# Linear-attention kernel: the value products cut into 64 by 32 pieces on eight array tiles, the state product's loops turned

## The chip, the cores and the metric

The kernel runs on one core of one Trainium2 chip. The metric is the device time of one execution in microseconds (us). The three runs of the kernel before took 1104.5, 1074.18 and 1075.11 us, median 1075.11 us. The profiled execution is a further run with its own time.

## The reference

The input is x of 8 sequences, 1024 tokens and 512 channels in fp32. The block is

```
x = x + attn(layernorm(x));   x = x + ffn(layernorm(x))
attn: q, k, v = split(x @ W_attn + b_attn), 16 heads of 32
      q = elu(q) + 1;  k = elu(k) + 1
      token by token:  kv += k_t (outer) v_t;  ksum += k_t
                       y_t = (q_t @ kv) / (q_t . ksum + 1e-6)
      return y @ W_proj + b_proj
ffn:  x and weight clipped to +-448 and rounded to fp8 e4m3, then x @ weight.T + bias
```

So attention is causal and linear: a token's output is its query times the running sum of the outer products of keys and values.

## The kernel before

**Tiling.** The 8192 tokens are 64 steps of 128 tokens (`NT` = 64, 8 steps to a sequence, `PER` = 8). Step n has two halves of 64 tokens, a = 0 and 1. A block is four steps; the projection to q, k and v of block j+1 is computed while block j's attention runs. The 16 heads stand as 4 groups g of 4 rows h: head 4g+h has its 32 channels on partitions 32h to 32h+31 of `qk[:, g, :]`.

**One step on TensorE (PE),** in the order that the loop at line 390 gives it: `scores(n)` (k times q within each half), `from_state(n)` (q times what was summed before the half: `state` for half 0, `mid` for half 1), two of the block-ahead projections of 12 matmuls each (`ahead`), four transposes of keys (`k_tokens(n+1)`), the third projection, `values(n)` (masked scores times v), `update(n+1)` (keys times values of the next step, into `mid` and `state`), `proj(n-1)`, `ffn(n-2)`. The last four steps (`tail(n)`) have no projection ahead.

**The small products.** Scores, state product, values and update are fp32. Each such matmul of the program stands in the profile as two LDWEIGHTS and two MATMUL instructions; the text calls one LDWEIGHTS with its MATMUL a pair. The array is cut into tiles by the partitions that the operands come from (rows) and those that the result goes to (columns):

| product | line | array tile | tiles in use | pairs in a step | columns streamed |
|---|---|---|---|---|---|
| scores | 305 | 32 by 64 | 8 | 64 | 64 |
| state product | 320 | 32 by 64 | 4 at a time (a is the outer loop) | 64, or 32 in a sequence's first step | 33 |
| values | 337 | 64 by 64 | 2 of 4 (half a from rows of half a to columns of half a) | 64 | 33 |
| update | 290 | 64 by 32 | 8, or 4 where only `mid` is made | 64 or 32 | 33 |

The 33rd column of v is 1, so that column 32 of each result is the denominator. `S` has four PSUM banks, one for each h; the scores of row h stand in its columns 0 to 255, and `Y`, the sums of state product and values, in columns 256 to 387 of the same bank. In every bank partition p of `Y` is token p of the step.

**After the values** DVE (line 640 to 650) adds 1e-6 to the denominators, takes the reciprocal and multiplies all of `Y` into `y`, in one instruction of 128 by 512; the next `scores` waits for it (`s_y`). ACT and POOL split `y` into two fp16 parts, and a transposing DMA brings them to `yt` for `proj`. After `proj` come DVE's sum and statistics (L661, L578 to L583), POOL's normalization (L838, L840), ACT's rounding to fp8 and a transposing DMA `x2t<-x2b` (L953), for which `ffn` waits. All DMAs are issued by SP in one order. The masks of the scores run on DVE (L618) and by ACT and POOL; `values` waits for both.

Almost all matmuls are recorded at line 212, the helper `matmul`, so they are told apart by their tiles.

Of the kernel before, what the change touches and what calls it, by code (L numbers as in the profile page):

```python
# [5 lines left out]
ALU = mybir.AluOpType  # L6
# [11 lines left out]
P = 128  # L18
HALF = P // 2
W = 33  # L20
# [28 lines left out]
def state_count(n):  # L49

    return n + 1 - (n + 1) // PER


def tail(n):
    return n >= NT - 4


def masked_dve(n):

    return n + 1 if not tail(n) else NT - 4 + 2 * (n - NT + 4) + 2  # L60
# [15 lines left out]
def build(nc, x_d, wa_d, ba_d, wp_d, bp_d, wf_d, bf_d, out_d):  # L76
    ctx = ExitStack()
    with ctx:
        def sb(name, shape, dt):
            return ctx.enter_context(nc.sbuf_tensor(name, shape, dt))  # L80
# [4 lines left out]
        def sem(name):  # L85
            return ctx.enter_context(nc.semaphore(f"s_{name}"))
# [10 lines left out]
        sm = sb("sm", [P, 4, 4, HALF], F32)  # L97

        state = sb("state", [P, 2, 4 * W], F32)
        mid = sb("mid", [P, 4 * W], F32)  # L100
        den = sb("den", [P, 16], F32)
        y = sb("y", [P, D], F32)
# [27 lines left out]
        Y = S[:, :, 4 * HALF:4 * HALF + 4 * W]  # L130
# [33 lines left out]
        s_mid, s_state, s_den, s_dinv, s_y, s_ytl = sem("mid"), sem("state"), sem("den"), sem("dinv"), sem("y"), sem("ytl")  # L164
# [20 lines left out]
        def parts(n):  # L185
            j, c = divmod(n, 4)
            return qk[j % 2], v1[j % 2], j, c

        def tokens(n, a):

            c = n % 4
            return slice(c * P + a * HALF, c * P + (a + 1) * HALF), slice(a * HALF, (a + 1) * HALF)

        block = ctx.enter_context(nc.Block())

        @block.tensor
        def _(e):
# [13 lines left out]
            def matmul(out, a, b, start, stop):  # L211
                return e.matmul(out, a, b, start=start, stop=stop, skip_group_check=True)  # L212
# [94 lines left out]
            def from_state(n):  # L307

                src, v, j, c = parts(n)
                first = n % PER == 0  # L310
                pe.wait_ge(s_mid, n + 1)
                if not first:
                    pe.wait_ge(s_state, state_count(n - 1))
                for a in range(1 if first else 0, 2):
                    cols, out = tokens(n, a)
                    held = mid if a else state[:, n % 2, :]
                    for g in range(4):
                        for h in range(4):
                            rows = slice(32 * h, 32 * h + 32)
                            mm = matmul(Y[out, h, g * W:(g + 1) * W], src[rows, g, cols], held[rows, g * W:(g + 1) * W],  # L320
                                        g == 0, False)
                            if a == 1 and g == 3:
                                mm.then_inc(s_score, 1)

            def values(n):
                src, v, j, c = parts(n)
                first = n % PER == 0
                pe.wait_ge(s_smd, masked_dve(n))
                if not tail(n):
                    pe.wait_ge(s_sel, n + 1)  # L330
                pe.wait_ge(s_v, n + 1)
                pe.wait_ge(s_one, 2)
                for h in range(4):
                    for g in range(4):
                        for a in range(2):
                            rows = tokens(n, a)[1]
                            mm = matmul(Y[rows, h, g * W:(g + 1) * W], sm[rows, h, g, :], v[rows, c, 4 * g + h, :],
                                        first and a == 0 and g == 0, True)
                mm.then_inc(s_av, 1)

            def t_y(n):
# [48 lines left out]
            for n in range(NT + 2):  # L390
                j, c = divmod(n, 4)
                if n < NT:
                    scores(n)
                    from_state(n)
                    ahead(j + 1, 3 * c)
                    ahead(j + 1, 3 * c + 1)
                if n <= NT and tail(n - 1):
                    t_y(n - 1)
                if n < NT:
                    if n + 1 < NT:  # L400
                        k_tokens(n + 1)
                    ahead(j + 1, 3 * c + 2)
                    values(n)
                    if n + 1 < NT:
                        update(n + 1)
                if 1 <= n <= NT:
                    proj(n - 1)
                if n >= 2:
                    t2(n - 2)
                    ffn(n - 2)  # L410
# [163 lines left out]
        def _(e):  # L574
# [59 lines left out]
            def values(n):  # L634

                out = Y.rearrange("p h (g w) -> p h g w", w=W)
                inv = den[:, :].rearrange("p (h g) -> p h g", h=4).unsqueeze(3)
                dve.wait_ge(s_av, n + 1)
                dve.wait_ge(s_y, n)
                e.tensor_scalar(inv, out[:, :, :, 32:33], DEN_EPS, None, ALU.add).then_inc(s_den, 1)  # L640
                dve.wait_ge(s_den, n + 1)
                e.reciprocal(den[:, :], den[:, :]).then_inc(s_dinv, 1)
                dve.wait_ge(s_dinv, n + 1)
                if tail(n - 1):
                    dve.wait_ge(s_ty, n - NT + 4)
                elif n:
                    dve.wait_ge(s_yl, n)
                    dve.wait_ge(s_yh, n)
                e.tensor_tensor(y[:, :].rearrange("p (h g i) -> p h g i", h=4, g=4), out[:, :, :, 0:32],  # L649
                                inv.broadcast_to([P, 4, 4, 32]), ALU.mult).then_inc(s_y, 1)  # L650

            def t_y(n):
                dve.wait_ge(s_yth, n - NT + 5)
# [149 lines left out]
            for n in range(NT + 2):  # L803
                j, c = divmod(n, 4)
                if n < NT:
                    if n + 8 < NT:
                        ln1(n + 8)
                    scores(n)
                    ahead(j + 1, 3 * c)
                    if n == 1:  # L810
                        ffn_sum()
                    if n + 8 < NT:
                        ln1_parts(n + 8)
                    ahead(j + 1, 3 * c + 1)
                if n <= NT and tail(n - 1):
                    t_y(n - 1)
                if n < NT:
                    if n == 0:
                        proj_weight()
                    ahead(j + 1, 3 * c + 2)  # L820
                    if n == 0:
                        ffn_high()
                    values(n)
                    if n + 1 < NT:
                        update(n + 1)
                    if n == 0:
                        ffn_round()
                if 1 <= n <= NT:
                    proj(n - 1)
                if n >= 2:  # L830
                    ffn(n - 2)
# [193 lines left out]
```

## Time and profile before

| | us |
|---|---|
| median of 3 runs | 1075.11 |
| profiled execution, its time | 1077.97 |
| profiled execution, its span | 1076.2 |
| PE busy | 1048.8 (97% of the span) |
| PE weight loads busy | 616.9 (57%) |
| DVE busy | 648.9 (60%) |
| ACT busy | 458.3 (43%) |
| POOL busy | 534.8 (50%) |

The granted clock of TensorE was 0.99 of full speed over the span. Busy time of PE is the time in which at least one matmul is under way; small matmuls overlap, so a stage's cost is read in the timeline, from its first start to the next stage's first start. In a timeline row the second number runs from the first start to the last end of the group.

### The profile page before, as it was taken

What the parts mean: (1) busy time and instruction counts of PE and PEld (TensorE: products, weight loads), DVE (VectorE), ACT (ScalarE), POOL (GpSimd) and SP (SyncE); (2) the same over time, 40 slices, a digit from 0 to 9 for tenths busy, and PEclk for the clock granted to TensorE, in tenths of its full rate; (3) what the DMA queues carried; (4) which work ended last, traced back from release to release, by engine and by line L of the source; (5) the groups of instructions that cost most, each with busy time, mean ns of one, the idle gap of its engine ahead of it and who ended that gap; (6) DMA issues with size and microseconds to landing.
All of it is one profiled execution on the core that took longest, in us unless ns stands there. A gap on an engine that the chain in (4) does not pass through costs nothing.

```text
span 1076.2 us, 43457 instructions
## 1 busy us (share of the span) xinstructions
PE 1048.8 (97%) x19504; PEld 616.9 (57%) x19504; DVE 648.9 (60%) x1319; ACT 458.3 (43%) x715; POOL 534.8 (50%) x524
## 2 busy tenths in 40 slices
PE   5989999999999999999999999999999999999996
PEld 3456555556556556556555555555555655655663
DVE  6666666666666566565665656566565656644454
ACT  5633452533534353452534444353452534434222
POOL 3445665554554454554455454455455455443233
PEclk9989999999999999999999999999999999999997
DMA  8615333333324324224333234333323433221121
GB/s 270 92 34 84 80 66 81 81 73 79 75 71 81 75 66 91 71 66 86 75 78 79 70 70 83 75 76 81 70 72 84 71 81 76 61 61 46 32 58 45
DMA packets 185354, 82.51 MB, mean 77 GB/s; under 512 B 165840, under 2 KB 165840, under 8 KB 185168
## 3 DMA queue, kind: packets, MB, share of 16 engines
q1 hardware_dynamic: 185168, 79.73, 33.5%
q8 instruction: 153, 2.51, 1.0%
q14 instruction: 33, 0.27, 0.1%
HBM read 22.81 MB, written 16.78 MB: 37 GB/s over the span
## 4 chain that ended last, share of the span: by engine, by line
PE 93%; DVE 2%; POOL 1%; ACT 1%; issue 1%; DMA 1%; POOLq 0%
PE R L212 70%; PE S L212 21%; PE R L216 3%; POOL st L838 1%; DVE st L578 0%; POOL xn L840 0%; DMA x2t<-x2b 0%; DVE xs L661 0%; DVE sm L618 0%; POOL xnhl L853 0%; DMA xs<-in_L_attn_x 0%; DVE wl L716 0%; DVE raw L755 0%; ACT qk L426 0%; ACT wh L417 0%
## 5 line engine op out<-in xcount | busy, mean ns | idle before, releaser
L212 PE MATMUL R<-xt,wh 128*128 128x512 f16 x1024 | 307.1, 382 | 2.4 <-ACT wh L417 2.4
L601 DVE SCALAR_TENSOR_TENSOR qk<-qk,rel 128x512 f32<-128x512 f32 x128 | 131.1, 1025 | 170.1 <-ACT rel L429 170.0
L872 POOL TENSOR_TENSOR yhl<-y,yhl 128x512 f16<-128x512 f32 x60 | 70.1, 1168 | 322.0 <-ACT yhl L417 322.0
L212 PE MATMUL R<-xt,wl 128*128 128x512 f16 x512 | 194.3, 381 | 0.0
L838 POOL TENSOR_TENSOR st<-st,half 128x1 f32<-128x1 f32 x128 | 94.1, 735 | 187.8 <-DVE st L583 175.3
L212 PE MATMUL R<-wh,xt 128*128 128x512 f16 x512 | 161.5, 382 | 0.0
L212 PEld LDWEIGHTS R<-xt,wh 128*128 128x128 f16 x1024 | 96.9, 98 | 108.7 <-DVE xt L709 2.6
L426 ACT ACTIVATE qk<-R,bqk,wm 128x512 f32<-128x512 f32 x128 | 99.5, 777 | 121.4 <-PE R L212 121.3
L212 PEld LDWEIGHTS S<-v,sm 64*64 64x64 f32 x4096 | 124.5, 135 | 28.6 <-issue 25.4
L212 PE MATMUL R<-wph,yt 128*128 128x512 f16 x512 | 132.9, 382 | 2.0 <-DVE yt L654 2.0
L212 PE MATMUL S<-v,sm 64*64 64x33 f32 x4096 | 131.6, 221 | 2.3 <-DVE sm L618 2.3
L661 DVE SCALAR_TENSOR_TENSOR xs<-R,wm,xs 128x512 f32<-128x512 f32 x64 | 48.1, 751 | 106.3 <-PE R L212 106.3
L417 ACT ACTIVATE yhl<-y 128x512 f16<-128x512 f32 x60 | 37.8, 631 | 165.5 <-DVE y L649 165.5
L860 POOL TENSOR_TENSOR xs<-xs,bp 128x512 f32<-128x512 f32 x64 | 107.3, 1682 | 0.0
L417 ACT ACTIVATE o<-R 128x512 f16<-128x512 f32 x64 | 38.2, 597 | 156.2 <-PE R L212 156.2
L429 ACT ACTIVATE rel<-R,bqk,wm 128x512 f32<-128x512 f32 x128 | 98.5, 769 | 0.0
L595 DVE TENSOR_TENSOR xnhl<-xn,xnhl 128x512 f16<-128x512 f32 x56 | 86.3, 1540 | 19.5 <-ACT xnhl L417 19.5
L212 PE MATMUL R<-wl,xt 128*128 128x512 f16 x256 | 97.7, 381 | 0.0
L578 DVE BATCH_NORM_STATS2 st<-xs 128x6 f32<-128x512 f32 x128 | 88.4, 691 | 6.2 <-DMA xs<-in_L_attn_x 3.9
L212 PEld LDWEIGHTS R<-xt,wl 128*128 128x128 f16 x512 | 50.4, 98 | 61.4 <-issue 1.7
L881 POOL TENSOR_TENSOR xs<-xs,bf 128x512 f32<-128x512 f32 x64 | 81.0, 1266 | 5.3
L212 PEld LDWEIGHTS R<-wh,xt 128*128 128x128 f16 x512 | 50.3, 98 | 56.4 <-issue 1.6
(90 smaller groups left out, 1440.7 us busy)
## 6 DMA issues: line engine op xcount, KB each, us to landing
xs<-in_L_attn_x SPq DMA_DIRECT2D x64, 256.0 KB, 3.4
out<-xs SPq DMA_DIRECT2D x64, 256.0 KB, 2.5
raw<-in_L_attn_W_attn SPq DMA_DIRECT2D x3, 1024.0 KB, 9.3
xs<-in_L_attn_W_proj SPq DMA_DIRECT2D x4, 256.0 KB
raw<-in_L_ffn_weight SPq DMA_DIRECT2D x1, 1024.0 KB, 16.4
x2t<-x2b SPq DMA_TRANSPOSE x62, 2.4
xt<-xnhl SPq DMA_TRANSPOSE x60, 3.2
yt<-yhl SPq DMA_TRANSPOSE x60, 3.3
```

The lines of the kernel that those rows point to most:

```text
L212: return e.matmul(out, a, b, start=start, stop=stop, skip_group_check=True)
L417: return e.activation(out, in_, ACT.Copy, **more)
L426: e.activation(dst[:, i, :], bank["qkv", j, i][:, :], ACT.Exp, scale=UN[i // 4], bias=bqk[:, i:i + 1])
L429: e.activation(rel[:, u % 2, :], bank["qkv", j, i][:, :], ACT.Relu, scale=UN[i // 4], bias=bqk[:, i:i + 1]).then_inc(s_relu, 1)
L578: e.bn_stats(row[:, 0:6], src).then_inc(s_bn, 1)
L595: e.tensor_tensor(xnhl[:, m % 4, 1, :], xn[:, m % 2, :], xnhl[:, m % 4, 0, :], ALU.subtract).then_inc(s_xlo, 1)
L601: e.scalar_tensor_tensor(qk[j % 2][:, i, :], qk[j % 2][:, i, :], 1.0, rel[:, (u - 1) % 2, :], ALU.min, ALU.add).then_inc(s_phi, 1)
L661: e.scalar_tensor_tensor(x, bank["proj", n][:, :], UN_P, x, ALU.mult, ALU.add).then_inc(s_x1, 1)
L838: e.tensor_tensor(row[:, 10:11], row[:, 9:10], half[:, :], ALU.pow).then_inc(s_rs, 1)
L860: e.tensor_tensor(x, x, bp[:, :], ALU.add).then_inc(s_xb, 1)
L872: e.tensor_tensor(yhl[:, n % 2, 1, :], y[:, :], yhl[:, n % 2, 0, :], ALU.subtract).then_inc(s_yl, 1)
L881: e.tensor_tensor(x, x, bf[:, :], ALU.add).then_inc(s_x1b, 1)
```

## The change

`values` cuts each product of 64 tokens by 64 columns of the array into two of 64 by 32, so it has 128 pairs in a step instead of 64. For the odd rows h = 1 and 3 the halves change places in `Y`: half 0's results go to partitions 64 to 127, half 1's to 0 to 63 (`valued`). Four groups of pieces in turn then use all eight tiles of 64 by 32. `from_state` writes to the same swapped places, and its loops are turned: g is outermost and the halves alternate within it, so that eight tiles of 32 by 64 are in use. DVE's multiplication, which has to bring the odd rows' halves back, becomes three instructions: one of 128 partitions by 256 elements for h = 0 and 2, and two of 64 partitions by 256.

```diff
+        def valued(a, h):
+            b = (a + h) % 2
+            return slice(b * HALF, (b + 1) * HALF)
...
-                for a in range(1 if first else 0, 2):
-                    cols, out = tokens(n, a)
-                    held = mid if a else state[:, n % 2, :]
-                    for g in range(4):
+                for g in range(4):
+                    for a in range(1 if first else 0, 2):
+                        cols = tokens(n, a)[0]
+                        held = mid if a else state[:, n % 2, :]
                         for h in range(4):
                             rows = slice(32 * h, 32 * h + 32)
-                            mm = matmul(Y[out, h, g * W:(g + 1) * W], src[rows, g, cols], held[rows, g * W:(g + 1) * W],
-                                        g == 0, False)
+                            mm = matmul(Y[valued(a, h), h, g * W:(g + 1) * W], src[rows, g, cols],
+                                        held[rows, g * W:(g + 1) * W], g == 0, False)
...
-                for h in range(4):
+                for h in (0, 2):
                     for g in range(4):
-                        for a in range(2):
+                        for a, i in ((0, h), (1, h), (0, h + 1), (1, h + 1)):
                             rows = tokens(n, a)[1]
-                            mm = matmul(Y[rows, h, g * W:(g + 1) * W], sm[rows, h, g, :], v[rows, c, 4 * g + h, :],
-                                        first and a == 0 and g == 0, True)
+                            for at in range(0, HALF, 32):
+                                out = valued(a, i).start + at
+                                mm = matmul(Y[out:out + 32, i, g * W:(g + 1) * W], sm[rows, i, g, at:at + 32],
+                                            v[rows, c, 4 * g + i, :], first and a == 0 and g == 0, True)
...
-                e.tensor_tensor(y[:, :].rearrange("p (h g i) -> p h g i", h=4, g=4), out[:, :, :, 0:32],
-                                inv.broadcast_to([P, 4, 4, 32]), ALU.mult).then_inc(s_y, 1)
+                dst = y[:, :].rearrange("p (h g i) -> p h g i", h=4, g=4)
+                e.tensor_tensor(dst[:, 0:4:2, :, :], out[:, 0:4:2, :, 0:32],
+                                inv[:, 0:4:2, :, :].broadcast_to([P, 2, 4, 32]), ALU.mult)
+                for a in range(2):
+                    at, to = valued(a, 1), tokens(n, a)[1]
+                    made = e.tensor_tensor(dst[to, 1:4:2, :, :], out[at, 1:4:2, :, 0:32],
+                                           inv[at, 1:4:2, :, :].broadcast_to([HALF, 2, 4, 32]), ALU.mult)
+                made.then_inc(s_y, 1)
```

## Rows read from the trace of the kernel before

**Rows 1.** The page: span, then line, engine, operation, tiles, count, busy us, mean ns, idle.

```profile
span 1076.2 us, 43457 instructions
...
PE 1048.8 (97%) x19504; PEld 616.9 (57%) x19504; DVE 648.9 (60%) x1319; ACT 458.3 (43%) x715; POOL 534.8 (50%) x524
...
PE R L212 70%; PE S L212 21%; PE R L216 3%; POOL st L838 1%; DVE st L578 0%; POOL xn L840 0%; DMA x2t<-x2b 0%; DVE xs L661 0%; DVE sm L618 0%; POOL xnhl L853 0%; DMA xs<-in_L_attn_x 0%; DVE wl L716 0%; DVE raw L755 0%; ACT qk L426 0%; ACT wh L417 0%
...
L212 PE MATMUL S<-v,sm 64*64 64x33 f32 x4096 | 131.6, 221 | 2.3 <-DVE sm L618 2.3
```

**Rows 2.** Timeline of PE, one step: start us, us until the group's last end, what.

```profile
499.88 2.06 PE L212 MATMUL S<-v,sm 64*64 64x33 f32 x64
501.86 0.76 PE L212 MATMUL R<-v,ktok 64*32 64x33 f32 x64
502.55 1.04 PE L212 MATMUL R<-wph,yt 128*128 128x512 f16 x4
```

**Rows 3.** Weight loads of S that began by a time, counted (x) from 499.80.

```profile
499.80:500.20 0.40, 0.33 (x12) 1.00 0.54 105
499.80:501.20 1.40, 1.33 (x46) 1.00 0.62 135
```

**Rows 4.** Timeline of PE in 0.07 us at the start of the values.

```profile
499.88 0.25 PE L212 MATMUL S<-v,sm 64*64 64x33 f32 x2
```

**Rows 5.** Weight loads of the update, counted (x) from 501.80.

```profile
501.80:502.01 0.21, 0.15 (x33) 1.00 1.09 146
501.80:502.16 0.36, 0.30 (x36) 1.00 0.86 137
501.80:502.31 0.51, 0.45 (x54) 1.00 0.71 120
```

**Rows 6.** Timeline of PE, scores and state product of the same step.

```profile
506.11 0.85 PE L212 MATMUL S<-qk 32*64 32x64 f32 x60
...
507.73 0.61 PE L212 MATMUL R<-xt,wh 128*128 128x512 f16 x2
```

**Rows 7.** Weight loads of S in that stretch, counted (x) from 506.10.

```profile
506.10:506.51 0.41, 0.40 (x37) 1.00 0.00 0
506.10:506.71 0.61, 0.60 (x61) 1.00 0.00 0
```

**Rows 8.** Timeline of PE, a sequence's first step, without the state.

```profile
184.29 0.91 PE L212 MATMUL S<-qk 32*64 32x64 f32 x64
185.00 0.67 PE L212 MATMUL S<-mid,qk 32*64 32x33 f32 x32
185.60 0.60 PE L212 MATMUL R<-xt,wh 128*128 128x512 f16 x2
```

**Rows 9.** Timeline of DVE behind the values.

```profile
501.98 0.18 DVE L640 TENSOR_SCALAR den<-S 128x16 f32<-128x16 f32 x1 [1.25 <-PE S L212]
...
502.48 0.69 DVE L649 TENSOR_TENSOR y<-S,den 128x512 f32<-128x512 f32 x1
...
503.40 0.30 DVE L632 TENSOR_TENSOR state<-R,mid 128x132 f32<-128x132 f32 x1
```

**Rows 10.** Issues of x2t over 490 to 990 us.

```profile
L953 SPq DMA_TRANSPOSE x2t<-x2b x31: 1188/1222/1232, 499.2 to 982.7; - x31
...
DMA to landing us min/median/max: 2.3/2.5/4.3
```

**Rows 11.** Timeline, an issue of x2t by SP, and the next ffn on PE.

```profile
516.72 1.22 SPq L953 DMA_TRANSPOSE x2t<-x2b  x1
...
521.32 1.03 PE L212 MATMUL R<-wft,x2t 128*128 128x512 bf16 x4
```

**Rows 12.** Timeline of PE, the last steps, and what ended its idle time.

```profile
1024.09 2.06 PE L212 MATMUL S<-v,sm 64*64 64x33 f32 x64 [0.78 <-DVE sm L618]
...
1029.78 1.04 PE L212 MATMUL R<-wft,x2t 128*128 128x512 bf16 x4 [0.24 <-DMA x2t<-x2b]
...
1033.81 2.06 PE L212 MATMUL S<-v,sm 64*64 64x33 f32 x64 [0.35 <-DVE sm L618]
```

## Prediction

> **What bounds the kernel now.** I read the page's engine totals first: PE is busy for 97% of the span, DVE for 60%, the others less, and the chain that ended last runs through PE's R and S products for over 90% [rows 1]. So the order of work on PE sets the time, and a stage is worth what lies between its first start and the next stage's first start. The group's busy time, 131.6 us for the values [rows 1], is not that price, since each burst's last 0.2 us is also counted. In the timeline of one step the values run from 499.88 to 501.86, 1.98 us, the update from there to 502.55, 0.69 us [rows 2]; scores and state product together run from 506.11 to 507.73, 1.62 us [rows 6]. The reader is to see that the values have 1.98 us of a step, and scores with state product 1.62 us; the other stages stay as they are.
>
> Next, what limits each burst. Counting weight loads that began by a time gives a pace. The values go at 34 pairs in 1.00 us, 29.4 ns each [rows 3]; with two tiles that is 58.8 ns per pair and tile. The state product alone, on four tiles (a sequence's first step), has 31 intervals in 0.67 - 0.22 us, 14.5 ns each [rows 8], again 58 ns per tile (0.22 us is one matmul's own time, as in [rows 1]). So a 64-column load with 33 streamed columns occupies its tile for 58 ns, and two or four tiles are too few. The update, on eight tiles, behaves otherwise: its 64 pairs are not held by their tiles. 33 loads begin within 0.15 us of the first at 501.86, then there is a pause, 36 are out at 0.30 us, and 18 more follow in 0.15 us, 8.33 ns each [rows 5]. The scores, on eight tiles of another shape, show the same: 37 at 0.40 us, 24 more in 0.20 us, 8.33 ns [rows 7]. Two shapes with one pace: I read this as PE's queue, which holds some 33 pairs while it waits, and is then refilled at 8.33 ns per pair. That is the new limit.
>
> **Part 1, values.** 64 pairs at 29.4 ns become 128 pairs at 8.33 ns, if eight tiles keep up. They should: in the update the same shape does 8.33 ns with eight tiles, so each tile takes a pair in 67 ns or less, and 33 loads went out in 0.15 us, 4.5 ns each. Load k then begins 0.30 + (k - 36) x 0.00833 us after the first. From the update's 64th load (0.30 + 28 x 0.00833 = 0.53 us) to the next stage 0.69 - 0.53 = 0.16 us pass [rows 2, 5]. There are two ways to close the sum. If the update stays as it is (0.69 us), the values take 0.30 + 92 x 0.00833 + 0.16 = 1.22 us, and the step gains 0.76 us. If values and update, now of one tile shape, run as one burst of 192 pairs, they take 0.30 + 156 x 0.00833 + 0.16 = 1.76 us against 2.67, a gain of 0.91 us. The update's first instruction carries waits in either case, so I take 0.85 us. Ends: 0.91 above; below, 0.36 us, if 128 pairs take as long as the 128 pairs of scores and state product do now, 1.62 us [rows 6]. A loss has a rival of its own.
>
> **Part 2, state product.** 64 pairs with the order of g and halves that the scores have, and their tiles. As one burst of 128 pairs with the scores: 37 at 0.40 us, 91 more at 8.33 ns make 1.16 us, plus 0.16 us, 1.32 us against 1.62: 0.30 us gained [rows 6, 7]. Its tile needs 58 ns for a pair and would be asked once in 8 x 8.33 = 67 ns, so it just fits. Below, nothing is gained if that fit fails. Seven steps of eight have both halves; in the first of a sequence only the four tiles of half 1 work, as now [rows 8], and nothing changes.
>
> **Part 3, DVE.** One multiplication of 512 elements took 0.69 us, an operation on 16 elements 0.18 us (rounded rows), so 256 elements should take 0.18 + 240 x 0.51/496 = 0.43 us, and three such 1.28 us: y comes 0.6 us later after the values' end [rows 9]. If an operation on 64 partitions or with displaced partitions had a penalty, I bound it by another 0.7 us, the present operation's own time. Behind it in DVE's order wait `mid` and `state` (ended 503.70) and the sum after `proj`. The reader of y on PE is `scores` at 506.11, 2.9 us behind y's end at 503.17 [rows 6, 9]. The window from the values' end to the scores does not shrink, since update, proj and ffn stay. So this costs nothing with either price, and `state`, needed at the state product, keeps over 1.5 us. If that cover were gone, up to 0.6 us a step would be due. ACT's and POOL's split of y and its DMA shift by the same 0.6 us, with a whole step of room.
>
> **Part 4, what becomes late.** No instruction of a DMA moves. But x2t for ffn hangs on PE events before the values (ACT gets to the rounding only after the key transposes), so shorter values bring ffn nearer to a landing that does not move. In the row shown SP issues at 516.72, the landing is due a median 2.5 us later at 519.2, and ffn starts at 521.32: 2.1 us of room, of which 0.85 goes. The slowest landing was 4.3 us, which leaves 0.3 us [rows 10, 11]. With the median at 2.5 and the longest at 4.3 I estimate that one step in five is late, by some 0.4 us: 60 x 0.2 x 0.4 = 5 us lost.
>
> **Part 5, the last four steps.** There are no projections ahead, and PE already waits: 0.78 and 0.35 us for the mask, 0.24 us for x2t [rows 12]. Step 60's gains end in a longer wait for x2t at 1029.78; in steps 61 to 63 the state product's gain ends in the wait for the mask, which follows DVE's chain after proj. Of the values' gain in those three (2.6 us) I keep 2 us.
>
> **The sum.** 60 steps x 0.85 = 51.0; state product in 60 - 8 = 52 steps x 0.30 = 15.6; tail 2; x2t -5; DVE 0. Together 63.6 us. From the profiled execution's 1077.97 us that gives 1014.4 us. The median of the runs shown is 1075.11, 2.9 us below it, so I forecast 1012 us as the kernel's usual time.
>
> **Rivals.**
>
> *The queue is refilled worse than that* (12%). After 33 quick pairs there is a pause of some 0.12 us, once in each burst today [rows 5]. Should it come back every 32 pairs, 192 pairs see four more (0.48 us) and scores with state product two more (0.24 us): 60 x 0.48 + 52 x 0.24 = 41 us less, 1053 us; with half of it 1032 us. For it: no burst at this pace beyond 64 pairs exists in the trace. Against: 60 pairs of scores pass with one pause [rows 7].
>
> *x2t becomes the limit* (7%). If the landings, crowded into shorter steps, all take 4.3 us, a usual step has 0.3 us of room and loses 0.55 us: 33 us in all instead of 5, hence 1040 us.
>
> *Only two tiles work at a time, and nothing is gained* (6%). The two pieces after each other share their rows and their half of a bank. If the next half's pieces did not start until these are through, the pace is that of two tiles; with loads of half the columns at half of 29.4 ns, 14.7 ns, 128 pairs take 1.88 + 0.16 = 2.04 us. Values unchanged, state product without its gain: 1075 us. The trace speaks against it: two value matmuls of different halves are under way within the first 0.05 us, in the same bank h [rows 4].
> The Trainium skill (TensorEngine Tiling (Array Packing), Restrictions and Gotchas) says that different row tiles cannot access the same PSUM bank at the same time. By that rule this rival would hold, because pieces of both halves go to bank h; the trace does not agree where the two results lie on different partitions, which is the case here too.
>
> *Slower: a piece costs what a product costs now* (6%). If the tile is held for 58.8 ns whatever the columns and two work at a time, 128 pairs take 128 x 0.0294 + 0.16 = 3.92 us instead of 1.98: 63 x 1.94 = 122 us more, 1197 us, or 1181 us with the state product's gain. It decides from a pace of (1.98 - 0.16)/128 = 14.2 ns per pair upward. For it: 29.4 ns is today's pace of exactly this stage [rows 3]. Against: the update's 8.33 ns with the same shape and the same 33 columns [rows 5].
> The Trainium skill (TensorEngine Tiling (Array Packing), Performance Considerations, Instruction Overhead) gives each matmul about 60 cycles of overhead, so that a small dimension should not be split; at 2.4 GHz that is an estimated 25 ns per instruction and would make the values 3.2 us. The update's row contradicts it for matmuls on different tiles.
>
> **Chances and range.** The forecast's own course has 69%, with 1000 to 1028 us: the upper gains (0.91 and 0.30 us everywhere, no loss at x2t) give 1075.11 - 54.6 - 15.6 - 2 = 1003 us and noise a little less, half of the state product's gain and 0.75 us for the values 1026 us. To hold 8 in 10 I take in half of the refill rival and the x2t rival's nearer part: 1001 to 1036 us. A measurement of this kernel tells about 2% from no change (1053.6 and 1096.6 us). Faster by more: 69 + 11 + 6 = 86%. Within 2%: the two-tile rival, the far ends of refill and x2t, 8%. Slower: 6%.
>
> **What would show it.** Right: values as MATMULs of 64*32, 128 in a step, with the proj's first start 1.75 to 1.9 us behind the values' first; weight loads at 8.33 ns beyond the 64th; scores with state product in 1.3 us except in a sequence's first step; three multiplications on DVE of about 0.43 us, PE not waiting for y; waits of ffn for x2t in a fifth of the steps. Wrong: a second pause in the bursts, a pace over 10 ns, PE idle before scores with y named, or waits for the masks before step 60.

## The result, and the profile after

The changed kernel took 1110.76 us, median of four runs (1108.34 to 1116.52), against 1074.64 us for the kernel before in the same session: ratio 1.0345, 95% interval 1.0296 to 1.0395. One run of the kernel before, of 1104.5 us, was in a slower state of the chip, and the ratio, taken from the means, leaves it out. The forecast was 1012 us, so it is slower where a gain was predicted. The profiled execution took 1111.12 us.

The page of the changed kernel, to be laid beside [rows 1]: span, engine totals, the chain by engine, and the queue that brings instructions. Before, that queue had 153 packets and 2.51 MB.

```profile
span 1109.4 us, 51715 instructions
...
PE 1014.3 (91%) x23538; PEld 571.2 (51%) x23600; DVE 684.7 (62%) x1447; ACT 459.6 (41%) x715; POOL 543.7 (49%) x524
...
q8 instruction: 185, 3.03, 1.2%
...
PE 81%; issue 7%; DVE 4%; DMA 3%; POOL 2%; ACT 2%; SPq 1%; POOLq 0%
```

PE's busy time fell by 34.5 us (1048.8 to 1014.3) as meant, but the span grew by 33.2 us. PE, busy for 97% before, is now idle for 95 us, and "issue" has grown to 7% of the chain, where it was 1%: there an engine waited for nothing that the profile shows. This share alone proves nothing, since the kernel on four tiles below has 7% too and hardly stands still; what counts are the waits of PE, further down.

A step that goes well, in PE's timeline of the changed kernel (start us, us to the group's last end), answers to [rows 2]:

```profile
513.71 1.43 PE L218 MATMUL S<-v,sm 64*32 64x33 f32 x128
514.99 0.87 PE L218 MATMUL R<-v,ktok 64*32 64x33 f32 x64
515.79 1.04 PE L218 MATMUL R<-wph,yt 128*128 128x512 f16 x4
```

Values and update take 515.79 - 513.71 = 2.08 us instead of 2.67. Scores and state product take 1.47 us instead of 1.62. The gain of such a step is 0.59 + 0.15 = 0.74 us. The values' weight loads, counted from 513.60, answer to [rows 3]:

```profile
513.60:514.11 0.51, 0.40 (x48) 1.00 0.00 0
513.60:514.51 0.91, 0.80 (x96) 1.00 0.08 15
```

48 loads in 0.40 us are 8.33 ns each, where it was 29.4 ns. This pace was forecast and is there, but not to the burst's end. The same count shows a second pause, after load 119:

```profile
513.60:514.71 1.11, 1.00 (x119) 1.00 0.25 52
513.60:514.82 1.22, 1.11 (x120) 1.00 0.33 67
```

One load began in this 0.11 us, and the next came 0.12 us behind it. A third pause, of 0.09 us, follows in the update, and the last of the 192 loads begins 1.93 us after the first, where the forecast's 0.30 + 156 x 0.00833 makes 1.60 us.

A step that goes badly, five steps later, same view:

```profile
594.17 1.41 PE L218 MATMUL S<-v,sm 64*32 64x33 f32 x128
595.44 0.85 PE L218 MATMUL R<-v,ktok 64*32 64x33 f32 x62
599.04 0.22 PE L218 MATMUL R<-v,ktok 64*32 64x33 f32 x2 [2.75 <-issue]
599.19 1.88 PE L218 MATMUL R<-wph,yt 128*128 128x512 f16 x4
600.86 1.91 PE L218 MATMUL R<-wpl,yt 128*128 128x512 f16 x4
602.57 1.07 PE L218 MATMUL R<-wph,yt 128*128 128x512 f16 x4
```

After 62 of the update's 64 matmuls PE stands still for 2.75 us, with its operands and semaphores ready: the last two belong to the same loop and wait for nothing of their own. Then four matmuls of the projection take 1.88 us where they took 1.04. The next fence shows the clock beside it. Its rows are stretches with PE, PEld, DVE, ACT and POOL busy, granted clock, DMA share and GB/s: the clock was 0.50 behind that idle stretch, the lower of its two levels, 1.2 instead of 2.4 GHz, and 1.00 throughout a clean step.

```profile
482.90:498.30 15.40, 15.35 (x376) 8.82 (x376) 9.58 (x22) 4.46 (x8) 8.31 (x8) 1.00 0.36 86
594.10:603.70 9.60, 6.80 (x206) 3.81 (x207) 3.07 (x10) 2.26 (x4) 1.16 (x1) 0.82 0.50 72
600.20:602.40 2.20, 2.20 (x7) 0.76 (x5) 0.00 (x0) 0.00 (x0) 0.00 (x0) 0.50 0.03 7
```

The DMA view of the same kernel between 587.5 and 596.6 us has no packet on the instruction queue; between 596.6 and 599.0 it has one:

```profile
q1 hardware_dynamic: 363, 0.27, 113.8%
q8 instruction: 1, 0.02, 2.4%
```

So PE had run out at 596.29, the packet came after that, and PE went on at 599.04. The waits of PE in the changed kernel (us in total, times, longest us), of which the first two have no counterpart in the kernel before:

```profile
PE R L218 <- issue: 53.0, 30, 2.9
PE S L218 <- issue: 4.7, 8, 1.1
PE R L218 <- DMA x2t<-x2b: 4.4, 7, 1.5
```

**The account.** From the values of step 2 to those of step 60 the kernel before took 926.7 us and the changed one 955.8, 29.1 us more. At 0.59 us in each of these 58 steps and 0.15 us more in the 51 that have both halves of the state product, they should have taken 42 us less, so some 71 us were lost. Of PE's idle time by issue 52 us lie in this stretch. Eight times in it the clock stood at 0.50 for 3.4 us, each time beside one of its 24 idle stretches of over 1 us; at half speed that costs at most 14 us. With 3 us of waits for x2t and 1 us for a mask these make 70 us. Undisturbed steps took 15.0 to 16.0 us, hit ones 16.3 to 20.0.

DVE's multiplications answer to [rows 9]: 0.42 us, then two in 0.85 us. After the first step PE never waited for y.

```profile
516.40 0.42 DVE L658 TENSOR_TENSOR y<-S,den 128x256 f32<-128x256 f32 x1
516.84 0.85 DVE L663 TENSOR_TENSOR y<-S,den 64x256 f32<-64x256 f32 x2
```

x2t landed later: median 3.8 us after its issue over 100 to 900 us, where it was 2.4 in the same stretch of the kernel before (2.5 in [rows 10]).

### The profile page after: what moved, and what is told of

It is laid out like the page before. It is cut to its first block, busy times and chain, and to the rows that moved or that the text cites. A ratio compares the mean times of both kernels' runs of the same rounds, so it can differ in the third digit from the quotient of the medians.

```text
span 1109.4 us, 51715 instructions
## 1 busy us (share of the span) xinstructions
PE 1014.3 (91%) x23538; PEld 571.2 (51%) x23600; DVE 684.7 (62%) x1447; ACT 459.6 (41%) x715; POOL 543.7 (49%) x524
## 3 DMA queue, kind: packets, MB, share of 16 engines
q1 hardware_dynamic: 185168, 79.73, 34.5%
q8 instruction: 185, 3.03, 1.2%
## 4 chain that ended last, share of the span: by engine, by line
PE 81%; issue 7%; DVE 4%; DMA 3%; POOL 2%; ACT 2%; SPq 1%; POOLq 0%
PE R L218 64%; PE S L218 15%; DMA x2t<-x2b 3%; PE R L222 2%; DVE xnhl L603 1%; SPq L952 1%; POOL st L853 1%; DVE st L586 1%; POOL xn L855 1%; ACT rel L437 1%; DVE xs L676 0%; DVE sm L626 0%; POOL xnhl L868 0%; POOL x L855 0%; ACT qk L434 0%
## 5 line engine op out<-in xcount | busy, mean ns | idle before, releaser
L609 DVE SCALAR_TENSOR_TENSOR qk<-qk,rel 128x512 f32<-128x512 f32 x128 | 125.5, 981 | 175.3 <-ACT rel L437 175.2
L218 PE MATMUL R<-wph,yt 128*128 128x512 f16 x512 | 141.7, 401 | 6.4 <-issue 4.4
L218 PEld LDWEIGHTS S<-v,sm 64*32 64x32 f32 x8192 | 82.7, 105 | 31.7 <-issue 27.3
L603 DVE TENSOR_TENSOR xnhl<-xn,xnhl 128x512 f16<-128x512 f32 x56 | 83.3, 1487 | 20.6 <-ACT xnhl L425 19.8
L218 PE MATMUL S<-v,sm 64*32 64x33 f32 x8192 | 91.2, 201 | 4.1 <-DVE sm L626 2.7
L218 PE MATMUL R<-v,ktok 64*32 64x33 f32 x3840 | 53.9, 201 | 44.4 <-issue 44.2
L880 POOL TENSOR_TENSOR sm<-sm,causal 128x512 f32<-128x512 f32 x60 | 86.9, 1448 | 0.0
```

The costliest lines, as they stand in the source:

```text
L603: e.tensor_tensor(xnhl[:, m % 4, 1, :], xn[:, m % 2, :], xnhl[:, m % 4, 0, :], ALU.subtract).then_inc(s_xlo, 1)
L609: e.scalar_tensor_tensor(qk[j % 2][:, i, :], qk[j % 2][:, i, :], 1.0, rel[:, (u - 1) % 2, :], ALU.min, ALU.add).then_inc(s_phi, 1)
L880: e.tensor_tensor(sm[:, 2:4, :, :], sm[:, 2:4, :, :], causal_over(2), ALU.mult).then_inc(s_sel, 1)
```

## The experiments

**The theory** (F): instructions reach PE in packets of 16 KB, that is 256 instructions or 128 pairs. A quick burst uses up what has been fetched before the next packet is there. Two counts carry the size: 185 packets with 3.03 MB are 16.4 KB each, and 3.03 MB for 23,600 pairs are 64 bytes per instruction; from packet to packet, over 100 to 1000 us, PE began on average 128.7 weight loads and semaphore waits (128.7 before, too), so about 128 pairs. **The rivals**: the swapped places or DVE's three operations (P), the earlier ffn and its wait for x2t (X), the turned tile order (T), eight 64 by 32 tiles on shared banks as such (C; the text on the moved projection calls this T).

### The state product alone

```diff
-                for a in range(1 if first else 0, 2):
-                    ...
-                    for g in range(4):
+                for g in range(4):
+                    for a in range(1 if first else 0, 2):
+                        ...
```

> Only the state product's loops are turned (g outside, the halves within); values, places in Y and DVE's multiplication are those of before. Theory F (instruction fetch: PE runs dry where a burst of quick pairs is longer than what has been fetched ahead, and the longest burst of the changed kernel, values and update, has 192 pairs): the longest burst stays at 128 pairs, so no new idle stretches; the stage of scores and state product goes from 1.62 to 1.47 us as in the changed kernel, 52 x 0.15 = 8 us, so 1067 us, ratio 0.993. Theory T (the turned order of tiles itself disturbs PE, for example by switching tiles more often): new idle stretches of PE with no releaser, over 1080 us.

Measured: 1068.15 us, ratio 0.9918 (0.990 to 0.9937). The stage took 1.47 to 1.48 us in nearly every full step, and PE's matmuls had no wait by issue. T falls, and this part of the change is a gain of 0.8%. Its size is half of the prediction's, 0.15 us and not 0.30.

### Four tiles instead of eight

```diff
-                            for at in range(0, HALF, 32):
-                                out = valued(a, i).start + at
-                                mm = matmul(Y[out:out + 32, i, g * W:(g + 1) * W], sm[rows, i, g, at:at + 32],
-                                            v[rows, c, 4 * g + i, :], first and a == 0 and g == 0, True)
+                            mm = matmul(Y[valued(a, i), i, g * W:(g + 1) * W], sm[rows, i, g, :],
+                                        v[rows, c, 4 * g + i, :], first and a == 0 and g == 0, True)
```

> The changed kernel with its places, its order of groups and its DVE work, but each value product again one of 64 by 64: 64 pairs on four tiles. F: four tiles at 58 ns each give 14.6 ns per pair, values 0.92 + 0.16 = 1.1 us instead of 1.28 in the changed kernel, and no burst is longer than 128 pairs, so few or no idle stretches by issue: 1077 - 60 x 0.88 - 8 = 1012 to 1025 us, ratio 0.94 to 0.955. Theory P (the swapped places or the three DVE operations cause the loss): still about 1110 us, idle stretches stay. Theory X (waits for x2t, from shorter values): as many waits for x2t as in the changed kernel or more, over 1050 us.

Measured: 1027.05 us, ratio 0.9542 (0.9524 to 0.956). PE's timeline of this kernel:

```profile
507.75 1.14 PE L218 MATMUL S<-v,sm 64*64 64x33 f32 x64
508.82 0.76 PE L218 MATMUL R<-v,ktok 64*32 64x33 f32 x64
```

Values take 1.07 us, less than the 1.28 us with twice the tiles: four tiles at 58 ns a pair need 14.6 ns, and there are half as many pairs to feed. Waits by issue fell from 57.7 us to 1.9. P falls, and so does X, since PE waited longer for x2t than in the changed kernel (8 us, loads included) and the time is 84 us shorter:

```profile
PE R L218 <- DMA x2t<-x2b: 14.4, 22, 1.1
PEld R L218 <- DMA x2t<-x2b: 6.4, 7, 1.4
```

The time lies 2 us above the range of F. What stayed above the sum were these 21 us of waits for x2t.

### The third projection between values and update

```diff
-                    ahead(j + 1, 3 * c + 2)
                     values(n)
+                    ahead(j + 1, 3 * c + 2)
                     if n + 1 < NT:
                         update(n + 1)
```

> The changed kernel with the third block-ahead projection (12 matmuls, 2.7 us) moved on PE from before the values to between values and update; the same instructions. F: bursts are now 128 and 64 pairs with 2.7 us of slow matmuls between, so the stretches of 1 to 3 us by issue inside the update mostly go: 1015 to 1045 us (up to 0.4 us a step may be lost to the masks, as values start 2.7 us earlier). Theory P or X (places, DVE, x2t): unchanged, 1100 us or more. Theory T (pieces on eight tiles as such): unchanged.

Measured: 1126.48 us, ratio 1.0458 (1.0419 to 1.0497). A miss. Splitting the burst at this place did not help:

```profile
557.76 1.17 PE L218 MATMUL S<-v,sm 64*32 64x33 f32 x115 [1.20 <-POOL sm L880]
561.71 0.35 PE L218 MATMUL S<-v,sm 64*32 64x33 f32 x13 [2.78 <-issue]
```

The values now waited for the mask (33.2 us in all) and then stood still inside their own 128 pairs. So the rule "up to 128 pairs in a burst are safe", on which the expectation rested, was wrong. My reading is that PE's instruction stream also stands at the wait for the mask, so that nothing is fetched ahead during it; no run isolates that.

### The update issued twice in the kernel before

```diff
-                for g in range(4):
+                for g in (*range(4), *range(4)):
                     for a in range(len(out)):
```

> The kernel before with the update's matmuls issued twice (same results written twice), nothing else: 64 slow value pairs, then a burst of 128 quick pairs. Without any fetch limit the second 64 pairs cost 64 x 8.33 ns = 0.53 us in 56 steps and half of that in 7, 32 us in all: 1107 us. F: quick bursts as long as one fetch of 16 KB; idle stretches by issue of 1 to 3 us appear in part of the steps, so 1120 to 1160 us. T, P and X: 1107 us, no idle stretches by issue inside the update.

Measured: 1155.22 us, ratio 1.073 (1.0701 to 1.0759), 48 us above the plain price of the pairs. PE's waits by issue were 30 us of them; the rest was not split up. Most updates of 128 pairs took 1.22 us, but some were broken off:

```profile
923.81 0.93 PE L212 MATMUL R<-v,ktok 64*32 64x33 f32 x76
926.12 0.34 PE L212 MATMUL R<-v,ktok 64*32 64x33 f32 x27 [1.38 <-issue]
```

The same stalls come without any part of the change, only from more quick pairs. C, P and X cannot make them here.

### Places and DVE work alone

```diff
-                for h in (0, 2):
+                for h in range(4):
                     for g in range(4):
-                        for a, i in ((0, h), (1, h), (0, h + 1), (1, h + 1)):
+                        for a, i in ((0, h), (1, h)):
```

(with the products of 64 by 64 and the state product's loops as before)

> The kernel before with the swapped places in Y and DVE's three multiplications, but the products of 64 by 64 and both loops in the order of before. F: no stage of PE changes and no burst grows; DVE's extra 0.6 us a step lies beside proj and ffn: 1075 us, same within 0.5%. Theory P (places or DVE work cost something): 1085 us or more, with PE waiting for y or for x2t.

Measured: 1042.7 us, ratio 0.9693 (0.9671 to 0.9715), where I expected no change. DVE's longer work costs nothing, as forecast, but the values fell to 1.39 us:

```profile
501.56 1.46 PE L218 MATMUL S<-v,sm 64*64 64x33 f32 x64
502.95 0.76 PE L218 MATMUL R<-v,ktok 64*32 64x33 f32 x64
```

The swap alone puts odd rows h on the other two tiles, and PE starts on them before it has begun all 16 pairs of the even row ahead of them in the program. The count of weight loads shows it, first here, then in the kernel before:

```profile
501.50:502.01 0.51, 0.45 (x24) 1.00 0.00 0
```

```profile
499.80:500.32 0.52, 0.45 (x16) 1.00 0.42 80
```

In 0.45 us two tiles at 58 ns a pair take the 16 pairs of one row; 24 loads need the next row's tiles too. That the order of the loops need not be changed for it was not foreseen.

### Half of the pieces

```diff
-                            for at in range(0, HALF, 32):
+                            for at in ((0, 32) if first and a == 0 else (0,)):
```

> The changed kernel, but of the two pieces of each value product only the first is computed (both only for half 0 in a sequence's first step), so half of the tokens' values are missing: 64 pairs of 64 by 32 on the same eight tiles and banks, values and update together 128 quick pairs instead of 192. F: the stretches by issue inside the update vanish, values take 1.28 - 64 x 0.0083 = 0.75 us, a step 14.9 us, 1000 us or less (960 to 1000, with x2t late more often). Theory C (eight tiles of 64 by 32 on shared banks stall PE as such): stretches of 2 to 3 us remain, in about half as many steps, over 1040 us.

Measured: 1019.36 us, between the two bounds. The values took 0.61 us on the same eight tiles and banks, 9.5 ns a pair with what follows. The matmuls of update and projection waited 2.1 us by issue, nearly all of it in one step, instead of 53.0 us; 4.1 us stay on the products in S, most of it within scores and state product; 22 us were waits for x2t. C falls, since it asked for stalls in half as many steps. The time missed F's upper bound by 19 us, and the waits for x2t are as long; the next but one run takes them away on four tiles.

### A shift of half a packet

```diff
+EXTRA = 16
...
+                for _ in range(EXTRA if m == 3 else 0):
+                    transposes(out, [xn[:, m % 2, k * P:(k + 1) * P] for k in range(4)])
                 transposes(out, [xn[:, m % 2, k * P:(k + 1) * P] for k in range(4)]).then_inc(s_t1, 1)
```

> The changed kernel with 128 more PE instructions at the start (64 transposes repeated before the first projection, same results), nothing else. F: instructions come in pieces of 256 (16 KB), so half a piece more moves the piece's border in every later step: other steps are hit than before (in the changed kernel steps 31 to 36, 40 to 45, 48 to 53 are and 16 to 22, 26 to 30 aren't), and the total moves by up to 30 us either way. Theories C, P, X: the same steps are hit, since data, waits and DMAs of each step are the same; the total is 5 to 8 us longer.

Measured: 1120.38 us, ratio 1.0409. The hit steps moved. First values of four steps in the changed kernel (steps 42 to 45), then of the steps 40 to 42 in the shifted one:

```profile
747.85 1.42 PE L218 MATMUL S<-v,sm 64*32 64x33 f32 x128
767.85 1.45 PE L218 MATMUL S<-v,sm 64*32 64x33 f32 x128
787.27 1.46 PE L218 MATMUL S<-v,sm 64*32 64x33 f32 x128
805.13 1.41 PE L218 MATMUL S<-v,sm 64*32 64x33 f32 x128
```

```profile
753.92 1.42 PE L219 MATMUL S<-v,sm 64*32 64x33 f32 x128
769.37 1.42 PE L219 MATMUL S<-v,sm 64*32 64x33 f32 x128
785.07 1.41 PE L219 MATMUL S<-v,sm 64*32 64x33 f32 x128
```

Steps of 20.00, 19.42 and 17.86 us there, of 15.45 and 15.70 here, and steps 40 to 46 were all clean. In return steps 16 to 21, clean in the changed kernel, took 17.3 to 20.0 us. Data, waits and DMAs of a step are the same in both. Counting PE's instructions up to the first value matmul, modulo 256, sorts the steps of both kernels: in steps 3 to 58 a step of over 16.3 us had it at 32 to 155, and of the steps at 156 to 255 and 0 to 31 none took that long. Not every step at 32 to 155 was hit: two of 28 in each kernel, at 38 and 70, took 15.3 to 15.4 us.

### x2t earlier, on four tiles

```diff
 ACT:
+                    if 2 <= n < NT - 4:
+                        t2(n - 2)
                     ahead(j + 1, 3 * c + 1)
...
-                if 2 <= n < NT:
+                if NT - 4 <= n < NT:
                     t2(n - 2)
 SP:
+                if n >= 2:
+                    t2(n - 2)
                 if n + 8 < NT:
                     t1(n + 8)
-                if n >= 2:
-                    t2(n - 2)
```

> The four-tile version (1027 us) with ACT's rounding to fp8 moved ahead of its second block-ahead work, and SP issuing x2t before xt: x2t lands about 2.5 us earlier. In the four-tile version PE waits 21 us in all for x2t. If those waits are what separates it from its sum: 1027 - 17 = 1010 us, ratio 0.94. If SP's order only moves the wait (xt or yt late instead): 1020 to 1030 us.

Measured: 1012.31 us, ratio 0.940 (0.938 to 0.9419), faster than both kernels. x2t landed a median 2.3 us after its issue, and PE's waits for it fell from 21 us to under 2.

### The border held at a good place, and at a bad one

```diff
+                more = 19 if n % PER == PER - 1 else 0 if n % PER == 0 else 3
+                for k in range(more):
+                    matmul(out[0][32 * (k % 4):32 * (k % 4) + 32, 0:W], ktok[0:HALF, n % 2, 32 * (k % 4):32 * (k % 4) + 32],
+                           v[0:HALF, c, k % 4, :], True, True)
...
                             matmul(S[out, h, g * HALF:(g + 1) * HALF], src[rows, 4 + g, cols], src[rows, g, cols], True, True)
+                            if n and n % PER == 0 and 8 * g + 4 * a + h < 19:
+                                matmul(S[out, h, g * HALF:(g + 1) * HALF], src[rows, 4 + g, cols], src[rows, g, cols], True, True)
```

The second kernel has 18 repeats of the four transposes at the start besides (the edit of the shifted kernel with `EXTRA = 18`).

> The changed kernel with more PE work, all of it repeats of pairs that write the same results: 6 pairs before each update, 38 before an update that makes only mid and among the scores of a sequence's first step. PE then has 768 instructions, three pieces of 256 (16 KB), from each value stage to the next, so a piece's border always falls at the same place of a step. By counting in the changed kernel and in the shifted one, every step was hit whose first value instruction stood 32 to 155 instructions into its piece, and none at 160 to 255 or 0 to 30, save a few by 1 us. Here it stands at 206 in every step from 2 on. F: no step is hit; although about 3% of pairs are added (some 10 us of work), the time falls from 1111 to 1035 to 1055 us. Any theory without the pieces: 1120 us.

> The same with 144 more instructions at the start (72 repeated transposes), so that the first value instruction stands at 94 of its piece in every step. F: nearly every step is hit and takes 17.4 to 20 us instead of 15.5: 1180 to 1260 us. Any theory without the pieces: the same as e9_clear within 10 us.

Measured: 1055.85 us, ratio 0.9822 (0.9789 to 0.9855), and 1254.49 us, ratio 1.1668 (1.1619 to 1.1718). The pages of the two, spans and PE's totals:

```profile
span 1054.0 us, 53431 instructions
...
PE 1010.9 (96%) x24396; PEld 579.4 (55%) x24458; DVE 693.3 (66%) x1447; ACT 457.9 (43%) x715; POOL 532.8 (51%) x524
```

```profile
span 1250.3 us, 53575 instructions
...
PE 1071.6 (86%) x24468; PEld 601.5 (48%) x24530; DVE 692.0 (55%) x1447; ACT 458.9 (37%) x715; POOL 534.6 (43%) x524
```

144 instructions at the start make 199 us. The first time lies 1 us above the range of F, the second within it. In the first kernel steps 1 to 58 took 14.8 to 16.0 us; in the second all of them took 17.3 to 20.3. The first does more work than the changed kernel and is 55 us faster. The waits of PE's matmuls by issue in it, beside 53.0 us in the changed kernel:

```profile
PE R L218 <- issue: 8.4, 14, 2.6
```

Only 2.5 us of these waits lie in steps 2 to 59; the others are in the last four, where nothing holds the border.

No rival predicts either number. The traces also hold a closer test. In the same count of PE's instructions modulo 256, the first load after each idle stretch of PE's loads that lasted over 0.8 us by issue stands at 193 or 194: all 30 of them in the changed kernel from 95 us on, all 27 in the shifted one, all 61 in this second kernel, and all 20 with the update issued twice. So PE stops where a packet ends, and F is shown.

## Why the prediction was wrong

**Where the limit lies now: right for a clean step only.** There PE's work set the time, values on eight tiles ran at 8.33 ns a pair between their pauses, the state product's turned loops gained, and DVE's work stayed hidden.

**Part 1, the burst of values and update: the step that failed.** It took the pace after the pause as one that lasts for 192 pairs. The rows behind it showed at most 64 pairs, and some 60 of the scores [rows 5, 7], and the supply of instructions behind them was put at nothing. They come by DMA, 16 KB at a time. Where the next packet was not there, PE stood for up to 2.9 us, and in a part of these places its clock then stood at half for 3.4 us. In the kernel before, 128 pairs of values and update were spread over 2.67 us; now 192 go in 2.08. With the border kept at a good place the same work takes 1055.85 us, and at a bad one 1254.49.

**The terms that were mis-sized.** Values and update gained 0.59 us in a clean step, not 0.85: values took 1.28 us and the update 0.80 us behind them. The two further pauses, 0.12 and 0.09 us, are most of what was missing to 1.76 us. Scores and state product came to 1.47 us, not 1.32: 0.15 us gained, and 0.30 forecast. Together 0.74 us of 1.15 us. These terms alone, 42 us less, would still have been a gain.

**The rivals.** The one that named the refill priced a return of the 0.12 us pause. The pause did return, twice in 192 pairs and not four times, but it costs a step 0.2 us. What made the kernel slower was another thing, which no rival named: a late packet costs mostly 1 to 3 us and at times the clock behind it. The rival's far end was 1053 us. The rival on the slower side, a piece that costs what a product costs, was refuted (9.5 ns a pair for the half pieces, 8.33 for all). The two-tile rival did not hold either: pieces of both halves went to bank h, on different partitions of it, at 8.33 ns a pair. The Trainium skill (TensorEngine Tiling (Array Packing), Restrictions and Gotchas) says that different row tiles cannot access the same PSUM bank at the same time. The trace does not agree for tiles that write different partitions.

**x2t.** The forecast of a fifth of the steps late was near for the changed kernel, 8 us of waits against 5, but by luck: it kept the median landing at 2.5 us, which became 3.8, and left out the stalls, which gave the landing room. Without them the waits were 21 us on four tiles, which an earlier issue removed.

**Open.** The traces bound how far ahead packets come. In all twelve, when a packet began to move PE had at most 299 instructions left to begin before that packet's first, and it began that first one no earlier than 2.15 us after the packet began to move. How a semaphore wait in PE's own stream holds a packet up is argued from the run with the moved projection, not shown. Why the idle stretch lasted 1.6 us in one step and 2.9 in another, with the border at the same place, was not separated. Why x2t's landings grew slower in shorter steps was not separated from the transfers beside it; the earlier issue alone brought the median to 2.3 us.

## What to carry to other kernels

Cutting matmuls into more tiles doubles the instructions as well as the tiles. Before it, count the instructions of the densest stretch of PE, compare them with the 256 that one packet brings and the time that PE takes over them with the 2.15 us or more that passed here from a packet's start to its first instruction, and ask what the tiles really need: here four tiles with half the instructions were faster in the stage (1.07 us against 1.28) and in the kernel (1027.05 us against 1110.76). Idle time of PE with "issue" as its releaser, in the middle of a loop whose operands are ready, was instruction supply here, and a few repeated instructions that move the border test it. A count of pairs alone is no safe limit: with half of the pieces, 128 quick pairs stalled in one step; with the update issued twice, in many.

## What the runs showed of the hardware

- Instructions reached PE in packets of 16 KB, 256 instructions, and PE stood still for up to 2.9 us where a packet came too late. Whether a step was hit depended on its first instruction's place in a packet (1055.85 against 1254.49 us).
- Beside 8 of 24 such stretches of over 1 us PE's granted clock fell from 1.00 to 0.50 for 3.4 us: four matmuls of 512 columns took 1.88 us instead of 1.04.
- PE started matmuls on free tiles ahead of the program's order: with the order of before and only the places swapped, 64 value pairs took 1.39 us instead of 1.99, and 24 instead of 16 loads began in the first 0.45 us.
- A fp32 weight load of 64 columns with 33 streamed columns held its tile for 58 ns on two tiles (29.4 ns a pair) and gave 14.6 ns a pair on four. Three kinds of burst on eight tiles, of two shapes, ran at 8.33 ns; that the stream of instructions sets this pace is a reading that no run isolates.
